# A graph-attention kernel: shorter chunk records and end flags, a mask of nine columns, late rows moved behind the loop, and loops left where the code puts them

## The reference

```
xn  = layernorm(x)
x1  = x + attention(xn, edges) + mix(xn)
out = x1 + ffn(layernorm(x1))         # top-1 of 8 experts, capacity 977 rows
```

```
sim  = q[dst] . k[src] / sqrt(32)
p    = exp(sim - max of sim over the edges of dst)
agg[dst] = sum(p * v[src]) / sum(p)
out  = agg @ Wo.T + bo
```

## Time and profile before

| | |
|---|---|
| median of the runs | 3414.16 us (3398.33 to 3420.25) |
| span of the profiled execution | 3391.7 us; the time around the span is not shown for it, the three runs lie 6.6 to 28.6 us above it |
| first gather to the last chunk's end | 326 to 2842 us |
| instructions on the engines | 39,656 |
| busy share | PE 66%, DVE 72%, ACT 29%, POOL 62% |
| TensorE clock granted, mean | 0.81 of full speed |

### The profile page before, as it was taken

How to read it: one execution, slowest core, us unless ns; L and a number is a source line. 1 busy time by engine, 2 the same in 40 slices (tenths; PEclk the granted TensorE clock), 3 DMA queues, 4 the chain that set the end, 5 groups by cost and what they waited for, 6 DMA issues and landing times. The chain is left out here.

```text
span 3391.7 us, 39656 instructions
## 1 busy us (share of the span) xinstructions
PE 2234.0 (66%) x9400; PEld 1780.7 (53%) x9401; DVE 2425.6 (72%) x3389; ACT 992.9 (29%) x4133; POOL 2116.8 (62%) x2220
## 2 busy tenths in 40 slices
PE   5681467666666677766787676555655552669998
PEld 4570355555555455554565554433434431569998
DVE  5672577786777777888888685877888883546665
ACT  2220345545454455530111110000000000435543
POOL 4347666566665666666666666666666664548776
PEclk9795688888887888888888777777777886579999
DMA  5745666666666666667777776666666653723341
GB/s 193 249 146 147 172 187 185 170 183 181 185 181 169 186 183 181 189 186 212 221 214 217 217 223 187 190 184 186 186 187 180 187 160 122 256 80 76 88 91 26
DMA packets 258235, 590.52 MB, mean 174 GB/s; under 512 B 49410, under 2 KB 135505, under 8 KB 257565
## 3 DMA queue, kind: packets, MB, share of 16 engines
q0 software_dynamic: 150480, 467.10, 49.6%
q1 hardware_dynamic: 97947, 109.47, 9.7%
q10 hardware_dynamic: 9296, 9.44, 0.8%
HBM read 519.05 MB, written 71.76 MB: 174 GB/s over the span
## 5 line engine op out<-in xcount | busy, mean ns | idle before, releaser
L972 POOL DMA_INDIRECT wide<-kv_d,arena x1099 | 1054.3, 959 | 594.9 <-issue 404.8
L1277 PE MATMUL ps<-wide,arena 128*128 128x264 f32 x2432 | 760.9, 475 | 380.3 <-issue 263.6
L1277 PEld LDWEIGHTS ps<-wide,arena 128*128 128x128 f32 x2432 | 566.9, 239 | 565.2 <-issue 312.8
L972 POOL DMA_INDIRECT arena<-kv_d,arena x539 | 516.7, 959 | 283.4 <-issue 168.4
L1380 DVE TENSOR_TENSOR arena<-wide,ps 128x2048 f32<-128x2048 f32 x153 | 349.2, 2283 | 270.5 <-issue 95.4
L1383 DVE TENSOR_REDUCE arena<-arena 128x64 f32<-128x2048 f32 x229 | 523.4, 2286 | 7.9
L1277 PE MATMUL ps<-arena 128*128 128x264 f32 x1216 | 368.0, 465 | 158.4 <-issue 101.9
L1277 PEld LDWEIGHTS ps<-arena 128*128 128x128 f32 x1216 | 277.6, 233 | 242.6 <-issue 117.7
L1416 DVE TENSOR_TENSOR wide<-wide,ps 128x2112 f32<-128x2112 f32 x152 | 356.8, 2347 | 16.7 <-remote 16.7
L135 PE MATMUL ps<-halves 128*128 128x256 f32 (+2 forms) x2304 | 361.1, 319 | 3.3 <-DVE halves L1650 1.6
L135 PEld LDWEIGHTS ps<-halves 128*128 128x128 f32 x2304 | 330.8, 192 | 31.0 <-POOL halves L1660 3.6
(11 more groups left out here) (313 smaller groups left out, 3099.5 us busy)
## 6 DMA issues: line engine op xcount, KB each, us to landing
wide<-kv_d,arena POOLq DMA_INDIRECT x1099
arena<-in_w SPq DMA_DIRECT2D x16, 1024.0 KB
kv_d<-wide SPq DMA_DIRECT2D x49, 260.0 KB
arena<-xn_d SPq DMA_DIRECT2D x98, 128.0 KB
arena<-kv_d,arena POOLq DMA_INDIRECT x539
hb_d<-arena SPq DMA_DIRECT2D x16, 516.0 KB
q_d<-wide SPq DMA_DIRECT2D x49, 128.0 KB
xn_d<-arena SPq DMA_DIRECT2D x7, 896.0 KB
```

The lines of the kernel that those rows point to most:

```text
L972: e.indirect_dma_start(out=kvb[k][:, j, :], out_offset=None, in_=kv_d, in_offset=bass.IndirectOffsetOnAxis(ap=ixb[k][:, j:j + 1], axis=0)) ...
L1277: m = e.matmul(psE[(k + 1) % 3][:, 0:264], ident, kvb[b][:, j, 256:ROW], start=(j == 0), stop=(j == J - 1))
```

## The change

1. **Records.** The table of chunks has rows of five 16-bit numbers instead of four: arrivals, place in the mask, end flag, place of the query, place of the indices. The places are computed ahead of the loop. ACT reads its three with one load; DVE reads three. CH, the table's length, is 300 instead of 414.
2. **Flags.** The end flag is 0 or 1 and belongs to the chunk at which all four engines do their step, so no engine shifts flags. Dividing, transposing, projecting and storing a tile all stand in the same chunk's body; in the chunks with `mix` ACT does it behind the normalising.
3. **Mask.** A chunk's mask has nine columns (J + 1) of the scores instead of eight. The ninth is 0, and -BIG at a tile's first chunk; adding it restarts the maximum. The branches for the restart go. The copy of the maximum into column J moves from ahead of the mask to behind the difference, and waits for it.
4. **ACT's order.** The query is copied for every chunk, ahead of the exponentials, and both wait for the product of the next chunk (`e_prod`); the wait for `e_d` and the signal `e_q` go. DVE learns of the new query by `e_e`. The indices are copied behind the exponentials.
5. **Late rows.** The code for nodes with over 64 neighbours moves behind the loops and starts a tile anew (`late_tiles`, `late_tile`, `late_row`).
6. **Loops.** All have one turn of six chunks in their body; `aligned` gives no place and no announcement of the closing branch, for DVE neither. SP's loads for `mix` use three buffers instead of two.

In the built program the loops have 122 (DVE), 230 (POOL), 218, 122 and 98 (ACT), 162, 164 and 122 (PE) instructions.

```diff
-CH = 414
+CH = 300
+MB = 72
+TW = 5
...
-            with e.Fori(0, MIX // 2):
-                for k in range(2 * RING):
-                    body(k % RING, mix=True, i=k)
+            with turns(MIX, True):
+                for k in range(RING):
+                    body(k, mix=True, i=k)
...
+        def aligned(e, kind, end, hint=False):
+            return nc.Fori(0, end, engines=(kind,))
...
             def body(k, mix=False, join=None, aux=False, i=0):
-                e.reg_add(g_, g_, 1)
-                at = val(e, g_, CH - 14)
-                shift()
-                e.load([w_], tabF[:, bass.ds(at * 4 + 2, 1)])
-                e.reg_mov(qb, qa)
-                e.load([qa], tabF[:, bass.ds(at * 4 + 3, 1)])
-                e.load([t6, w6, p6], tabF[:, bass.ds(at * 4 + 4 * RING - 1, 3)])
-                e.wait_ge(e_prod, g_)
-                e.activation(ixb[k], ixf[:, bass.ds(val(e, p6, (NT + 1) * BLK - J) + val(e, t6, NT * BLK) * 4 + 256, J)],
-                             ACT.Copy).then_inc(e_ix, 1)
-                with e.If_ne(qa, qb):
-                    query()
-                with e.Else():
-                    e.nop().then_inc(e_q, 1)
-                e.wait_ge(e_d, g_)
+                record()
+                e.wait_ge(e_prod, gn)
+                query()
                 e.activation(p_ps, Db[:, 0:8 * J], ACT.Exp)
                 e.activation(alpha[k], D3[:, J, :], ACT.Exp).then_inc(e_e, 1)
-                with e.If_cmp(w1_, 1, "IS_GT"):
-                    slow_tile(e, "a_", tf, ns, one)
-                    e.reg_add(tf, tf, 1)
+                indices((k + 1) % RING)
                 if mix:
                     take_raw()
...
-                tile_end()
                 if mix or (join is not None and i < 2):
                     normalise(kv_sb[i % 2])
+                tile_end()
...
+            def record():
+                e.reg_add(g_, g_, 1)
+                e.reg_add(gn, gn, 1)
+                e.load([f_, qa, ix_], tabF[:, bass.ds(val(e, g_, CH - 14) * TW + 2, 3)])
...
             def body(k):
-                step()
+                record(k)
...
                 e.wait_ge(e_e, cg)
                 e.tensor_tensor(kvv[b], kvv[b], p3.unsqueeze(3).to_broadcast([128, J, 8, 33]), ALU.mult).then_inc(e_pv, 1)
-                with e.If_eq(w_, 0):
-                    e.tensor_copy(S3[:, J, :], peak)
-                with e.Else():
-                    with e.If_eq(w_, 2):
-                        e.tensor_copy(S3[:, J, :], peak)
-                    with e.Else():
-                        restart()
                 e.wait_ge(e_red, cg)
-                e.tensor_tensor(S3[:, 0:J, :], S3[:, 0:J, :], m_now.unsqueeze(2).to_broadcast([128, J, 8]), ALU.add).then_inc(e_mask, 1)
+                e.tensor_tensor(S3[:, 0:J + 1, :], S3[:, 0:J + 1, :], m_now.unsqueeze(2).to_broadcast([128, J + 1, 8]), ALU.add
+                                ).then_inc(e_mask, 1)
                 e.wait_ge(e_mask, cg)
                 e.tensor_reduce(peak, S_ps.rearrange("p (j h) -> p h j", h=8), AX.X, ALU.max).then_inc(e_max, 1)
                 e.wait_ge(e_max, cg)
                 e.tensor_tensor(D3, S3[:, 0:J + 1, :], peak.unsqueeze(1).to_broadcast([128, J + 1, 8]), ALU.subtract).then_inc(e_d, 1)
+                e.wait_ge(e_d, cg)
+                e.tensor_copy(S3[:, J, :], peak)
                 fade(k)
-                scores((k + 1) % RING, cn, ar)
+                scores((k + 1) % RING, cn, arr)
...
-            with nc.Fori(0, val(e, cnt_), engines=(mybir.EngineType.DVE,), head_slot={mybir.EngineType.DVE: 0}):
+            with aligned(e, mybir.EngineType.DVE, val(e, cnt_), hint=False):
                 for k in range(RING):
                     body(k)
```

More of the change, by code:

```diff
@@ L168, in gps_layer_kernel @@
         alpha = [take(8) for _ in range(RING)]
-        msave = [take(8) for _ in range(RING)]
+        permc = take(1).bitcast(i32)
         S_sb = take(8 * (J + 2))
@@ L601, in tables @@
             t_i = v(V.tensor_copy(nth[:, 0:128], iota))
-            for i in range(1, 4):
+            for i in range(1, 3):
                 n_ = min(128, CH - 128 * i)
@@ L870, in gps_layer_kernel, with rounds, turns @@
         UNITS = 2 * NT
-        def rounds(e, pre, body, step, between, aux=AUX):
+        def aligned(e, kind, end, hint=False):
+            return nc.Fori(0, end, engines=(kind,))
+        def rounds(e, pre, body, step, between, aux=AUX, kind=None):
+            def turns(end, hint=False):
+                return aligned(e, kind, end, hint) if kind is not None else e.Fori(0, end)
             (cnt_,) = regs(e, pre, ["cnt"], [1])
@@ L881, in rounds @@
             between[0]()
-            with e.Fori(0, aux):
+            with turns(aux):
                 for k in range(RING):
@@ L885, in rounds, with late_tiles, late_rows @@
             between[1]()
[L886 removed]
+            with turns(val(e, cnt_)):
                 for k in range(RING):
                     body(k)
[L890 to L892 removed]
+        def late_tiles(e, ns, tl, tile):
+            e.reg_mov(tl, 0)
+            e.reg_load(ns, nsl[0:1, 0:1])
             with e.While(lambda: val(e, ns) > 0):
[L894 removed]
+                e.reg_add(ns, ns, BLK)
+                tile()
+                e.reg_add(tl, tl, 1)
+                e.reg_load(ns, nsl[0:1, bass.ds(val(e, tl, NT), 1)])
+        def late_rows(e, ns, row_):
+            with e.While(lambda: val(e, ns) > 0):
+                row_()
                 e.reg_add(ns, ns, -1)
@@ L922, in mix_in @@
                 e.reg_add(w, w, 128)
-            for i in range(2):
+            for i in range(3):
                 mix_in(i)
-            with e.Fori(0, NT // 2 - 1):
-                for i in range(2):
+            with aligned(e, mybir.EngineType.SP, NT // 3 - 1):
+                for i in range(3):
                     e.wait_ge(e_kv, used)
@@ L985, in body, with late_row @@
                             fetch(j)
-                    with e.If_eq(end, 1):
-                        slow_tile(e, "g_", tf, ns, one)
-                        e.reg_add(tf, tf, 1)
-            def one():
+            def late_row():
                 e.reg_add(so, so, 1)
@@ L1273, in body @@
                         e.reg_add(xw, xw, 32)
-                e.load([w_], tabF[:, bass.ds(val(e, cg, CH - 14) * 4 + 2, 1)])
+                with e.If_eq(f_, 1):
+                    turn(k)
                 e.wait_ge(e_pv, cg)
@@ new lines, in record, with total, tile_end @@
+            def record(k):
+                e.reg_add(cg, cg, 1)
+                e.reg_add(c6, c6, 1)
+                e.load([arr, p, f_], tabF[:, bass.ds(val(e, cg, CH - 14) * TW, 3)])
+            def total(k):
+                e.wait_ge(e_fr, c6)
+                e.tensor_tensor(acc, acc, psE[(k + 1) % 3][:, 0:264], ALU.add).then_inc(e_sc, 1)
+            def tile_end(k):
+                with e.If_eq(f_, 1):
+                    e.reg_add(tf, tf, 1)
+                    e.wait_ge(e_sc, cg)
+                    divide(mo[k % 3], e_fin)
@@ new lines, in _ @@
+            (cnt_,) = regs(e, "v_", ["cnt"], [1])
+            e.reg_load(cnt_, nsl[0:1, 62:63])
+            with aligned(e, mybir.EngineType.DVE, val(e, cnt_), hint=False):
+                for k in range(RING):
+                    body(k)
+            for k in range(2):
+                record(k)
+                total(k)
+                tile_end(k)
+                link(e.memset(sp_[:, 64:65], 0.0))
+                fade(k)
+                e.wait_ge(e_al, cg)
+                e.nop().then_inc(e_dm, 1)
@@ L1438, in _ @@
-            (cnt_,) = regs(e, "v_", ["cnt"], [1])
-            e.reg_load(cnt_, nsl[0:1, 62:63])
-            with nc.Fori(0, val(e, cnt_), engines=(mybir.EngineType.DVE,), head_slot={mybir.EngineType.DVE: 0}):
-                for k in range(RING):
-                    body(k)
-            for k in range(2):
-                step()
-                e.reg_mov(w_, 0)
-                total(k)
-                tile_end(k)
-                link(e.memset(sp_[:, 64:65], 0.0))
-                e.nop().then_inc(e_dm, 1)
-                fade(k)
+                e.reg_add(sg_, sg_, 16)
```

372 lines of the change are left out of this document (183 added, 189 removed).

## The result

The changed kernel takes **3383.0 us** (median of 8 runs, 3375.9 to 3394.7); the kernel before took 3411.8 (8 runs, 3394.1 to 3420.3) on the same chip. The ratio is **0.9934, 95% interval 0.9909 to 0.9960**: 0.7% faster, within the 1% that the prediction called no change. Forecast were 3200 and a range of 3080 to 3400; 3383 lies inside the range, where of the forecast and its rivals only D puts it.

What follows compares the result with a forecast made beforehand. It took DVE's pace of 1894 us plus waits, mainly on ACT, to bound the loop, above POOL's floor of 2064. Terms -78 - 165 + 25 + 2 = -216 gave 3200 us, range 3080 to 3400.

Steps and rivals of the forecast that it cites:

- Rival D: DVE's product waits move to PE or gathers; closings and copy count at most: 3360 to 3410 us, 14%.
- the sentence on the floor: Attention loop: falls from 2500 to about 2290 us, above POOL's gather floor of 2064, so POOL doesn't cut the gain.
- DVE's closings, -78: Branch closing DVE's turn of six chunks: 35 waits of about 2.5 us before the total go, -78 us.
- rival C: DVE's loop without a place misses its branch target, so the closings' gain is lost: 3278 us, 8%.
- ACT's steps, -165: ACT's loop: about ten instructions instead of twenty per chunk without an end; -165 of DVE's 419 us product waits.
- PE's sums are late once ACT isn't: Attention loop: a named sign that the forecast is wrong, PE's sums being what is late; no size given.
- Exponentials behind the product, 0: ACT's exponentials, now after the next product: hidden by DVE's sum and total, 0 us.
- rival A: Exponentials arrive late at DVE's weighting; over 200 us of waits there would show it: 3430 to 3530 us, 10%.
- The maximum's copy, +25,: DVE's copy of the maximum, now behind the difference: 0.11 us more in each of 229 chunks, +25 us.
- Ends of tiles, 0: PE and ACT at a tile's end: PE waits for ACT's normalising, six buffers cover it, 0; far end 147 us.
- Tables, 0: Ahead of the loop: new table and mask work hides in DVE's wait of 47.62 us, 0 us.
- Rival B: ACT hardly ever last in spells, POOL's gathers set the loop's end: 2990 us, 12%.

Runs made afterwards that it cites:

- run 18: Kernel before, table read as unsigned numbers, never-run late-row code removed on DVE alone (458 to 182 instructions): 3407.1 us, ratio 0.9992, chip with spells.
- run 9: The changed kernel as it is, on a chip without spells: 2970.5 us beside 2987.0 for the kernel before, ratio 0.9943.
- run 8: Kernel before, table read as unsigned numbers, never-run late-row code removed on POOL, ACT and DVE: 2970.4 us, ratio 0.9952, chip without spells.
- run 15: Changed kernel with DVE's loop placed at the start of an instruction block as before the change: 2975.4 us, ratio 0.9957, chip without spells.
- run 3: Changed kernel with ACT's exponentials taken ahead of the next product again: 3393.3 us, ratio to the kernel before 0.9953, chip with spells.
- run 1: Changed kernel with the hand-overs at a tile's end spread over chunks again: 3417.9 us, ratio to the kernel before 1.0032, chip with spells.
- run 14: Changed kernel with the hand-overs at a tile's end spread over chunks again, on a chip without spells: 2977.5 us beside 2989.1, ratio 0.9964.
- run 12: Changed kernel with one more two-input 128 x 2048 product on DVE per turn of six chunks: 3035.2 us, ratio 1.0158, chip without spells.
- run 7: Changed kernel with one more one-input DVE operation per turn of six chunks: 2996.5 us, ratio to the kernel before 1.0042, chip without spells.

## Why the prediction was wrong, step by step

The step that failed is the sentence on the floor with the sum behind it: that the loop, at 2290 us still above 2064, is not cut by POOL, so that waits taken off DVE come off the time. It treated 508 us of waits as separate items. They are the share that reaches DVE of spells in which PE or ACT crawls until POOL stops for want of a buffer. Shown is that the edits left POOL's idle time and the span nearly where they were (the table), that DVE's waits moved instead of going (run 18: 564 and 560 us), and that without spells POOL never waits for a buffer (run 9). That a spell's length is set by POOL's running out is read from the timing of PE's spells and stays argued. The wait of ACT behind the last chunk fits it by its length, 33 us where there was nothing to run out of, but it ended before POOL's series did. What starts a spell is open.

1. *DVE's closings, -78.* Size right, worth wrong. 88 us left their place in run 18, 88 in the changed kernel; of them nothing came to the end with spells (run 18, at most 9 us by its interval), and without spells DVE's and the other engines' shorter bodies together gave 15 (run 8), POOL being the floor. The unplaced loop didn't miss (33 packets; run 15): rival C is out.
2. *ACT's steps, -165.* Mis-sized and misread. The waits that go by ACT fell from 444 (419 at the product, 25 at the weighting) to 384, by 60, and PE's at the total came to 81. Terms 1 and 2 together were to take 243 us off DVE's waits; the sum over the three places fell by 46, from 552 to 506. That a spell with fewer steps of ACT to hit hits PE, whose 32 instructions a chunk had stayed, is an inference; PE was hit before too, by the count above in 17 spells of 149 us, now in 23 of 206. "PE's sums are late once ACT isn't" was named as what would make the forecast wrong, and it is what the profile shows.
3. *Exponentials behind the product, 0.* Right in time, though the waits did move to the weighting. The prediction's mark for rival A, over 200 us there, was met (384) and the mark was bad: run 3 removed A's cause and the weighting waited longer (441). Where a wait stands says which signal comes last, not what makes it late.
4. *A query for each chunk, 0.* Right: ACT has 951 us of idle time before it.
5. *The maximum's copy, +25,* and 6. *nine columns, +2.* 8.40 instead of 8.27 us in a quiet chunk, +0.13 x 229 = 30. Right; without spells it is hidden, since DVE waits 122 us for gathers.
7. *Ends of tiles, 0.* Right for the time, for a reason not given. The chain is there (101 us at one chunk in five of the output stretch), yet taking it away made the kernel slower with spells (run 1) and changed nothing without (run 14).
8. *Tables, 0.* DVE's wait ahead of the loop rose from 47.6 to 49.5, and the first product stands 9 us later. Small, unforeseen.

Rival D, the gain given back to PE and to gathers at 3360 to 3410, held at 14%. It deserved more: rows 6 and 8 showed spells that ended when POOL paused, and that was set down without asking what POOL's pauses are then worth. Rival B is odd: its 2990, with POOL as what sets the end, is within 20 us the time on chips without spells, of both kernels. The profile of before could not show that such a chip exists.

## What to carry to other kernels

Before waits on one engine are subtracted, add up the idle time of the engine that feeds the ring and ask what ends it: here its pauses came ahead of the end of the slow stretches, and nothing saved downstream shortened them. A single edit that removes one stall alone (run 18) is the cheapest test of whether stalls are items or shares of something else. And time a kernel on a second chip before explaining a tenth of its time: 12% of this one's belonged to the chip it was profiled on.

## What was not expected of the hardware

- **Chips differ on the same program, the quick ones by 12% of the others' time.** The kernel before took 3407 to 3412 us in three groups of runs and 2986 to 2989 in three others, each with runs within 1%. With the spells the granted clock was 0.79 over the changed kernel, without them 0.863; that isn't what made PE late, since its 2432 products of `L1286` in the two pages took 450 ns each with the spells and 457 without. What a spell is stays open. It isn't a lack of bandwidth as such: without spells the same gathers moved 217 to 220 GB/s in the slices of the stretch with `mix` and no step was slow, with them 172 to 188. Nor is it seen loading of code: the changed kernel has 33 packets of it on this queue in the whole execution, on either sort of chip. The three runs with half the bytes all met chips without spells.
- **A wait that had long been answered took 33 us** (ACT, 2803.4 to 2836.4 above), with POOL issuing without pause before and after its end.
- **A DVE operation on SBUF alone held up the gather beside it.** Timeline of run 12:

```profile
649.13 1.01 POOL L998 DMA_INDIRECT wide<-kv_d,arena  x1 [0.30 <-issue]
...
650.37 2.29 DVE L1403 TENSOR_TENSOR arena<-arena 128x2048 f32<-128x2048 f32 x1
650.44 3.04 POOL L998 DMA_INDIRECT wide<-kv_d,arena  x1 [0.30 <-issue]
...
652.69 2.29 DVE L1356 TENSOR_TENSOR arena<-wide,ps 128x2048 f32<-128x2048 f32 x1
653.79 0.95 POOL L998 DMA_INDIRECT wide<-kv_d,arena  x1 [0.30 <-issue]
```

The gather that starts beside it takes 3.04 us instead of 0.95; the kernel's own product, of the same length with one input in PSUM, leaves the next one at 0.95. In run 12 the mean of the 1099 gathers rose from 957 to 1013 ns, 62 us, nearly all of the 65 us that it was slower; in run 7, whose one-input operation ran in 1.22 us, from 957 to 981, 26 us, all of it. The Trainium skill, "GPSIMD Engine Reference", section "Key points", says that GpSimd shares its SBUF interfaces with VectorE and contends with its instructions in a 2-port performance mode or with two SBUF inputs. The trace of run 12 agrees, with 2.1 us for one gather. The operation of run 7 has one input and cost a gather 0.75 us (1.70 instead of 0.95); that it ran in a 2-port mode no run shows.
